# Flamingo layer on one core: weight units stored from ScalarE's queue, one tile prepared per turn, quarter-tile stores, another order of down products, scatters of the next group first

## The reference, cut to what matters

```python
# x, ctx: 32 sequences of 128 tokens, width 512, float32
xn = layernorm(x)
q  = rms_norm(xn @ Wq.T + bq) * nq            # 16 heads of 32
k  = rms_norm(ctx @ Wk.T + bk) * nk
v  = ctx @ Wv.T + bv
x  = x + tanh(g0) * (softmax(q k^T / sqrt(32)) v @ Wo.T + bo)

h  = layernorm(x)
s  = relu(h @ up) ** 2 @ down                 # 512 -> 2048 -> 512
m  = (h @ expert) * (sum of the 2 largest of h @ gate)
x  = x + tanh(g1) * (layernorm(s + m) * gamma + beta)
```

## Time and profile before

| | us |
|---|---|
| median of 3 runs | 1365.26 |
| lowest, highest | 1364.36, 1367.47 |
| the profiled execution | 1362.92 |
| its span | 1361.1 |
| attention part | 0 to about 566 |
| feed-forward, first products to end | about 566 to 1361 |
| last result of DVE | 1351.2 |

### The profile page before, as it was taken

One profiled execution on the slowest core, in us unless ns is written; L12 is line 12 of the kernel. 1 busy time (PEld: TensorE's weight loads), 2 busy tenths in 40 slices (PEclk: granted clock), 3 DMA queues, 4 the chain that ended last, 5 costly groups with the idle time before them and its releaser, 6 DMA issues.

```text
span 1361.1 us, 26319 instructions
## 1 busy us (share of the span) xinstructions
PE 1277.8 (94%) x9154; PEld 1093.8 (80%) x9154; DVE 943.1 (69%) x1568; ACT 755.8 (56%) x2012; POOL 591.3 (43%) x720
## 2 busy tenths in 40 slices
PE   7999999999899999999999999899999899999993
PEld 5887777777777778788899888799888789887993
DVE  6777777777766876665598665697664896366676
ACT  5877777777666757656455343454343543444440
POOL 3766666666655996463034322043311233111033
PEclk9999999999899999999999999899999999999997
DMA  6588888988878864659675687675677664564861
GB/s 226 140 211 222 220 221 222 231 221 213 218 200 196 205 153 115 228 220 237 233 238 177 225 234 221 202 227 176 239 227 223 220 188 165 193 221 153 230 184 62
DMA packets 335460, 276.96 MB, mean 203 GB/s; under 512 B 233852, under 2 KB 248316, under 8 KB 330239
## 3 DMA queue, kind: packets, MB, share of 16 engines
q1 hardware_dynamic: 297600, 165.79, 45.1%
q10 hardware_dynamic: 37758, 109.85, 24.6%
HBM read 198.79 MB, written 76.81 MB: 202 GB/s over the span
## 4 chain that ended last, share of the span: by engine, by line
PE 49%; DVE 16%; DMA 11%; SPq 7%; issue 6%; POOL 5%; ACT 3%; DVEq 0%; POOLq 0%; ACTq 0%
PE wide L79 15%; PE wide L80 14%; PE wide L81 14%; DMA kd_scratch<-kf 6%; SPq L1649 4%; DVE wo_lo L2006 4%; DMA k_dealt<-kd_scratch 3%; PE wide L418 2%; DMA out_x<-fxy 2%; ACT prob L817 1%; PE wide L406 1%; DVE S L1990 1%; POOL fxy L1447 1%; POOL prob L988 1%; PE wide L1728 1%
## 5 line engine op out<-in xcount | busy, mean ns | idle before, releaser
L817 ACT ACTIVATE prob<-wide,nmx 128x128 f32<-128x128 f32 x512 | 180.7, 396 | 6.0 <-DVE nmx L626 5.9
L988 POOL TENSOR_TENSOR prob<-prob,rr 128x512 f32<-128x512 f32 x128 | 136.1, 1075 | 103.9 <-DVE rr L634 103.9
L79 PE MATMUL wide<-eight,wo_hi 128*128 128x256 f32 x480 | 138.0, 288 | 12.5 <-DVE wo_lo L2006 8.3
L1820 ACT ACTIVATE hid<-wide 128x512 f32<-128x512 f32 x96 | 57.4, 599 | 156.6 <-PE wide L81 156.6
L80 PE MATMUL wide<-eight,wo_hi 128*128 128x256 f32 x480 | 136.4, 284 | 0.0
L81 PE MATMUL wide<-eight,wo_lo 128*128 128x256 f32 x480 | 136.3, 284 | 0.0
L2006 DVE TENSOR_TENSOR wo_lo<-hid,wo_hi 128x512 fp32r<-128x512 f32 x120 | 94.6, 810 | 43.6 <-ACT wo_hi L1820 43.6
L817 ACT ACTIVATION_READ_ACCUMULATOR prob<-wide,nmx 128x1 f32 x512 | 121.1, 236 | 0.0
L1820 ACT ACTIVATE wo_hi<-hid 128x512 fp32r<-128x512 f32 x120 | 74.4, 631 | 79.2 <-PE wide L81 79.2
L79 PE MATMUL wide<-wq_hi,eight 128*128 128x512 f32 x192 | 82.9, 432 | 27.1 <-DVE eight L565 27.1
L79 PEld LDWEIGHTS wide<-eight,wo_hi 128*128 128x128 f32 x480 | 92.8, 193 | 16.3 <-issue 9.4
(11 more groups left out here) (308 smaller groups left out, 3971.0 us busy)
## 6 DMA issues: line engine op xcount, KB each, us to landing
eight<-down_scratch ACTq DMA_DIRECT2D x32, 1024.0 KB, 8.0
wk_hi<-down_scratch ACTq DMA_DIRECT2D x12, 1024.0 KB, 7.8
wk_lo<-down_scratch ACTq DMA_DIRECT2D x12, 1024.0 KB, 7.5
wk_hi<-up_scratch ACTq DMA_DIRECT2D x12, 1024.0 KB, 6.8
eight<-up_scratch ACTq DMA_DIRECT2D x12, 1024.0 KB, 5.8
wk_lo<-up_scratch ACTq DMA_DIRECT2D x12, 768.0 KB, 5.6
eight<-up_scratch ACTq DMA_DIRECT2D x12, 768.0 KB, 7.0
xin<-in_x SPq DMA_DIRECT2D x32, 256.0 KB, 3.4
```

The lines of the kernel that those rows point to most:

```text
L79: eng.matmul(dst, ah, bh, start=first and k == 0, stop=False, skip_group_check=onto)
L817: i = act.activation(prob[par][:, g, h * P:(h + 1) * P], cols(bank[g], h), ACT.Exp, bias=nmx[:, n:n + 1], scale=1.0, accum_out=rs[:, n:n + 1])
L988: pool.tensor_tensor(p, p, r, ALU.mult).then_inc(po_p, 1)
L1820: return act.activation(dst, src, ACT.Copy)
```

## The change

1. **Unit stores.** SP no longer stores units. ACT does, in two parts: the raw quarters (3 of 7) at the start of the even slot, ahead of the last exponentials of the slot before, and the sums (4 of 7) at its end, after the high part of x. Semaphores are apart for the two (`st_q`, `st_qs`). Down: 2 and 2 DMAs, up: 4 and 4.
2. **First group.** One tile per slot: loads in slots 19 to 26 (four quarter DMAs each), statistics in 20 to 27, normalisation in 21 to 28 and now on DVE. Pair sums stay in slots 26 to 29, in another order. POOL keeps the reciprocal root.
3. **Groups.** SP in a group g > 0: `load_x(g+1)` first, residual tiles, seven deals, then store and residual of tiles 0 and 1, the eighth deal, tiles 2 and 3, then the four others. The statistics of the next group move from q = 1, 2 to q = 0, 1, the normalisation from 3, 4 to 2, 3; statistics of y to q = 4 to 7; results 0 to 3 to q = 5, 6.
4. **Quarter tiles.** Output stores, residual loads and the load of `last_res` are four DMAs of 32x512 in place of one of 128x512, and there is one semaphore per output tile. For the last group SP stores the first two quarters of each tile and ACT the other two.
5. **Down products.** Operand order is hid0, squared hid2, S2, S1, hid1, S4, hid3; S4 is formed in `hid`, at the steps of `SUM4_AT`, and `SUMS_AT` and `HI_AT` are later. Arithmetic and counts are the same.
6. **End.** For the last group DVE adds the epsilon to the variance and POOL only takes the power.

```diff
@@ slot on SP, on ACT
-                    if ff.third_of(s, par) is not None:
-                        ff.unit_store(sp, ff.third_of(s, par))
+                    if ff.third_of(s, par) is not None:
+                        ff.unit_store_raw(act, ff.third_of(s, par))
...
+                    if ff.third_of(s, par) is not None:
+                        ff.unit_store_sums(act, ff.third_of(s, par))
@@ slot on DVE, on POOL
+                    if ff_turn(s, TILE_DONE, ff.TILES) is not None:
+                        ff.normalise(dve, 0, ff_turn(s, TILE_DONE, ff.TILES))
+                    if ff_turn(s, TILE_STATS, ff.TILES) is not None:
+                        ff.stats(dve, 0, ff_turn(s, TILE_STATS, ff.TILES))
...
-                            ff.inv_std(pool, 0, tile)
-                            ff.normalise(pool, 0, tile)
@@ store_out
-        eng.dma_start(ff.dealt_rows(out[g * GB + i]), y[i]).then_inc(ff.st_o[i % HB], DMA)
+        for src, dst in ff.quarters(y[i], out[g * GB + i]):
+            eng.dma_start(dst, src).then_inc(ff.st_o[i], DMA)
@@ weigh
-            at_least(act, ff.st_o[j % HB], 2 * g * DMA)
+            at_least(act, ff.st_o[j], g * KT * DMA)
@@ fill_b on DVE
-                for tile in {1: range(HB), 2: range(HB, GB)}.get(q, ()):
+                for tile in {STATS_AT(g): range(HB), STATS_AT(g) + 1: range(HB, GB)}.get(q, ()):
                     ff.stats(dve, g + 1, tile)
@@ tables
-    SUMS_AT = (28, 30, 32, 34)
+    SUM4_AT = (20, 22, 24, 26, 28, 29, 30, 32)
+    SUMS_AT = (34, 37, 40, 42)
+    Y_AT = {4: (0, 1), 5: (2, 3), 6: (4, 5), 7: (6, 7)}
+    def STATS_AT(g):
+        return 1 if g == 0 else 0
```

More of the change, by code:

```diff
@@ L1396, in quarters, with load_consts @@
         return [(tile[m * P // KT:(m + 1) * P // KT, :], rows.rearrange("(b c) n -> c b n", c=KT)[m]) for m in range(KT)]
+    TILES, PAIRS = (2, 3, 0, 1, 6, 7, 4, 5), (2, 3, 0, 1)
     def load_first(sp, n):
-        if n == 0:
+        if TILES[n] == 0:
             sp.wait_ge(ql, 2 * NU)
+        if TILES[n] == 6:
             sp.wait_ge(st_q, UNITS_STORED)
[L1402 to L1410, removed]
+            sp.wait_ge(st_qs, UNITS_STORED)
+        for dst, src in quarters(y[TILES[n]], x2_dram[TILES[n]]):
+            sp.dma_start(dst, src).then_inc(ld_x[TILES[n] % HB], DMA)
+    def load_consts(sp):
+        sp.wait_ge(ga_zeroed, 1)
+        sp.dma_start(ga[:, :, 0:NE], t["gate"].rearrange("p (k n) -> p k n", k=KT)).then_inc(ld_g, DMA)
+        for src, dst in (("gamma", gamma), ("beta", beta)):
+            sp.dma_start(dst[:, :], t[src].broadcast_to([P, D])).then_inc(ld_g, DMA)
     def x_tile(g, tile):
@@ L1633, in store_out, with store_half @@
         eng.wait_ge(ff.dv_o, GB * g + i + 1)
-        eng.dma_start(ff.dealt_rows(out[g * GB + i]), y[i]).then_inc(ff.st_o[i % HB], DMA)
+        for src, dst in ff.quarters(y[i], out[g * GB + i]):
+            eng.dma_start(dst, src).then_inc(ff.st_o[i], DMA)
+    def store_half(eng, i, half):
+        eng.wait_ge(ff.dv_o, GB * LAST + i + 1)
+        for src, dst in ff.quarters(y[i], out[LAST * GB + i])[2 * half:2 * half + 2]:
+            eng.dma_start(dst, src).then_inc(ff.st_o[i], DMA)
     @block.sync
@@ L1685, in group @@
                         ff.piece_load(sp, q + 5)
-                if g > 0 and q in (2, 5):
-                    for i in range(2 * (q // 5), 2 * (q // 5) + 2):
-                        store_out(sp, g - 1, i)
-                        load_res(g - 1, i + HB)
-                if more and q in (4, 5):
-                    for tile in range(HB * (q - 4), HB * (q - 3)):
-                        deal(g + 1, tile)
+                if q in (4, 5):
+                    for tile in range(HB * (q - 4), HB * (q - 3)):
+                        deal(1, tile)
@@ new lines, in first_group, with later_group @@
+            ff.piece_store(sp, NQ)
+            ff.piece_store(sp, NQ + 1)
+        def later_group(g):
+            more = g < LAST
+            if more:
+                load_x(g + 1)
+            for i in range(HB):
+                load_res(g - 1, i)
+            if more:
+                for tile in range(GB - 1):
+                    deal(g + 1, tile)
+            for i in range(HB):
+                store_out(sp, g - 1, i)
+                load_res(g - 1, i + HB)
+                if more and i == 1:
+                    deal(g + 1, GB - 1)
+            for i in range(HB, GB):
+                store_out(sp, g - 1, i)
@@ L1693, in group @@
+        for g in range(NG8):
             if g == 0:
[L1694 to L1699 removed]
+                first_group()
+            else:
+                later_group(g)
+            if g < LAST:
                 for i in range(GB):
                     fetch(g + 1, i)
[L1702 to L1705 removed]
@@ L1707, in _ @@
-        for g in range(NG8):
-            group(g)
-        for i in (0, 1, 2, 3, 4, 6):
-            store_out(sp, LAST, i)
-        for n in range(HB):
-            sp.wait_ge(ff.st_o[n], 2 * NG8 * DMA)
+        sp.wait_ge(ff.pe_E, GB * NG8)
+        for i in range(GB):
+            for dst, src in ff.quarters(res(LAST, i), x2_dram[LAST * GB + i]):
+                sp.dma_start(dst, src).then_inc(ff.ld_r[i % HB], DMA)
+        for i in range(GB):
+            store_half(sp, i, 0)
+        for n in range(GB):
+            sp.wait_ge(ff.st_o[n], NG8 * KT * DMA)
@@ L1785, in down_part @@
             return mm3(pe, bank[m % 2 * HB + j][:, 0:H], [(hi[:, cols], lo[:, cols])], [(w[:, 0:H], w[:, H:D])],
-                       first=q == 0 and m in (0, 1, 5), last=q == NQ - 1, onto=m in (2, 3, 4, 6))
+                       first=q == 0 and m in (0, 1, 3), last=q == NQ - 1, onto=m in (2, 4, 5, 6))
         def last_product(g):
@@ L1944, in _ @@
             group(g)
-        store_out(act, LAST, 5)
-        store_out(act, LAST, 7)
+        for i in range(GB):
+            store_half(act, i, 1)
     @block.vector
@@ L2161, in group @@
                     ff.expert_lo(pool, NQ, ff.u_b)
+            if g > 0:
+                for i in range(HB, GB):
+                    residual(g - 1, i)
             if g < LAST:
```

194 lines of the change are left out of this document (101 added, 93 removed).

## The result

| | before | after |
|---|---|---|
| median of four runs each, us | 1365.9 | 1301.7 (1300.9 to 1305.3) |
| span of the profiled execution, us | 1361.1 | 1300.2 |
| first gate products of groups 0, 1, 2, 3, us | 587.6, 776.5, 972.9, 1169.2 | 539.0, 734.0, 929.1, 1116.7 |
| last gate to end of span, us | 191.8 | 183.5 |

The ratio is 0.9535, with an interval of 0.9513 to 0.9556. The kernel is faster by 64 us where 38 were forecast; the span, which the sum was made against, is 60.9 shorter. The forecast of 1327 had the direction, and the time fell out of the range of 1312 to 1347 at the fast end.

What follows compares the result with a forecast made beforehand. PE, busy 94% of the span, was taken as the bound, so its waits are time. Terms -24.4 - 6 + 2 - 15 + 14 - 2 - 6.5 = -37.9 took 1365.3 to 1327.4 us; 8-in-10 range 1312 to 1347.

Steps and rivals of the forecast that it cites:

- Unit stores: Attention: moving them to ACT's queue shortens ten slot pairs from 34.64 to 32.2 us, 24.4 us saved.
- PE would give two odd slots, 31.76: Attention: PE's bound for a pair of slots, taken as two odd slots of 15.88 us.
- The second bound: Attention: DMA engines have 29.5 us of work a pair and reach a share of 0.92, so 32.0 us.
- stands behind 1.75 MB on SP's queue: Attention, even slots: why the deal of `kf` takes 7.41 us; the unit store is ahead of it.
- a rival to which the forecast gave 0.05: Attention: ACT is blocked at its store issues, pairs last 37.8 us, time 1383 us; chance 0.05.
- The DMA engines give nothing: Attention: rival that the queue change saves only SP's issue time, 5 in place of 24.4 us, time 1347; chance 0.19.
- First group: Preparation, one tile per slot: 6 us saved in slots 26 and 27, 2 charged for DVE's added work.
- `weigh`: Feed-forward groups 1 and 2: its wait goes, 7.45 + 7.4 = 15 us saved; rival that it stays, 1342, chance 0.10.
- SP is through with seven deals before q = 5: Groups 1 and 2: scatters first finish before the first two results are ready, helping save 15 us.
- Statistics at q = 0: Groups 1 and 2: PE stalls 5.7 and 4.1 us, 14 lost with clock; no-stall rival 1313, chance 0.13.
- Down products: Feed-forward: spreading the sums cuts PE's waits for DVE, 2 us saved in all, between 0 and 8.
- The end: Last output store: 3.3 us in place of 9.9 saves 6.6; with DVE's small costs, 6.5 taken.

Runs made afterwards that it cites:

- e2: Kernel after with all four unit stores issued by SP again, at once, just ahead of the deal of kf: 1348.2 us, 0.9862.
- e1c: Kernel before with all four stores of a unit issued by ScalarE together at the slot's start: 1350.3 us, 0.9899.
- e1: Kernel before with only the unit stores moved to ScalarE, raw half at the slot's start and sums half later: 1321.8 us, 0.9676.
- e2c: Kernel after with unit stores on SP but spread, raw half ahead of the deal of kf, sums half last in the slot: 1311.7 us, 0.9592.
- e8: Kernel after with the old order of the seven down products and old places of the fourth and turned sums: 1310.9 us, 0.9585.
- e10: Kernel after with later groups' work in its old order, but quarter stores, per-tile semaphores and product order as changed: 1286.9 us, 0.9437.
- e7: Kernel after with ScalarE's first write to an output tile waiting for the stores of both tiles of the old pair: 1303.6 us, 0.9532.
- e6: Kernel after with each output tile stored by one DMA again, one semaphore per tile kept: 1312.4 us, 0.9597.
- e3: Kernel after with the next group's statistics at q = 1 and 2 and normalisation at q = 3 and 4 in every group: 1287.0 us, 0.944.
- e5: Kernel after with every store of a down unit written a second time, into an unread spare area: 1336.9 us, 0.9808.

## Why the prediction was right and wrong

**Unit stores: wrong size, and a mechanism that was right in part.** The forecast took 32.2 us for a pair, 24.4 in all; the store move alone brought 41.0 to gate 0. The step that failed is "PE would give two odd slots, 31.76". An odd slot's 15.88 us were not PE's work for a slot: PE did 150 matmuls in it and 116 in the even one, so a cut at SP's deals does not divide PE's work evenly; the kernel after, with no deal late, still has 149 and 120. A slot without a store has 15.09 us of work, with 131. The rows allowed a better sum: PE is busy for 15.88 + 16.07 = 31.95 us in the pair, and a granted clock of 0.91 over 18.39 us is up to 1.66 us of full speed lost. That gives 30.3, and 30.21 was measured. The second bound, a share of 0.92 as the most that the DMA engines reach, failed as well: they show 1.01, and up to 285 GB/s.

The mechanism, that the deal of `kf` "stands behind 1.75 MB on SP's queue", holds as far as this: the deal took 7.41 us to land there, 6.1 in e2 (at 200.64), and 3.3 in the kernel after. But it is not the whole of it. The rest is near a rival to which the forecast gave 0.05: an engine is held at its issues. SP was held at `x_dealt` for 4.35 us before, and DVE waited 3.22 us for that tile and then 1.42 us for `k_dealt`; the two are not separated. ScalarE was held too where it issued all four stores in a row (e1c). So the gain hangs on the store being split, spread over the pair and kept from right ahead of the deal, and little on the engine that issues it. No run has the whole burst right ahead of the deal but on the other queue, so whether the deal was late by its place in the queue or by the bytes beside it stays open. The 1.2 us of issues charged at nothing were rightly hidden: the profile of after shows the two issues of a half at 0.38 and 0.41 us, and beside ScalarE's 12.8 us of idle time at issues from 60 to 470 us PE waits for 2.5 us in all.

**The DMA engines give nothing, 0.19: refuted**, by e1. The sentence of the Trainium skill that was weighed with it ("DMA: Bandwidth & Descriptors", Issuing engines are not separate DMA queues), that another issuer saves only the time to start the DMAs, would have given 5 us. The measured 44 decide against that use of it, though not against what it says. Most of the 44 come from splitting and spreading the stores and not from the other issuer: with all of them on SP but spread, three quarters of the gain stay (e2c).

**First group: net 4 forecast, some 7.6 measured.** The step that was off is the 6 us for slots 26 and 27: the last six slots fell by 10.1 us from e1 to the kernel after. POOL is busy for 12.92 us in the slot that had 17.92, as forecast. The 2 us charged for VectorE's work beside the unit work were due, and the four slots with both grew by 3.6.

**`weigh`: the gain came as forecast, its reason was wrong.** Without the stall the intervals 1 to 2 and 2 to 3 are 9.8 and 8.6 shorter than before; 7.45 and 7.4 were forecast, and the products account for 0.4 and 1.1 us of the rest (e8). But the step "SP is through with seven deals before q = 5" is not needed (e10), and neither is the tile's own semaphore (e7) or the quarter stores (e6). Each of these runs keeps the two other edits, so any two of the three are enough. No run has one of them alone, so which of them would be enough by itself stays open.

**Statistics at q = 0: right mechanism, and nearly the size.** Stalls of 5.7 and 4.1 us were forecast and 6.0 and 6.8 came, with the clock 14 against 17 by the intervals (e3), inside the bound of 20. Group 2 was missed by 2.7 us: the step took 9.0 us for the landing of the last load, and the longest of that group now takes 11.8, so VectorE's last wait ends 15.0 us after `collect` and not 12.2. What slows the load is not shown; the step had named the residual loads, which now stand right behind it on SP.

**Down products: 2 forecast, 6.0 measured** (e8), inside the bounds of 0 to 8. PE's waits for these low parts fell from 8.3 us in the kernel before to 1.8. I had seen some 8 of them and taken most of the gain back for the stretch behind, and no new wait of PE of that size arose there.

**The end: 6.5 forecast, 6.7 measured**, 9.9 to 3.2.

Of the 23 us between -37.9 and -60.9 of span, 16.6 are the stores, 3.6 the first group, 4 the products and 2 the weighing; 3 more of stall go the other way. These are single executions: see the scatter of gate 0 at the end, which is as large as the smaller of these terms.

## What to carry to other kernels

To bound what a freed stretch will last, take PE's busy time over the whole pattern (both slots of the pair), less what a reduced clock accounts for, and not one part of it, since a cut between the parts need not divide PE's work evenly. Before moving large DMAs to another engine, ask how many stand in a row and what stands behind them: two at a time cost nothing here on ScalarE, 10 us in all on SP ahead of the deal (e2c), and four in a row held ScalarE for 3 us each time. Work that waits for fresh loads does not belong ahead of the operation that PE needs next: one constant in the changed kernel, undone, gives 1287.0 us, the fastest here with the old order of the later groups (1286.9).

## What the runs showed of the hardware

- Four DMAs of 384, 384, 512 and 512 KB in a row took ScalarE 0.38, 0.38, 0.66 and 1.42 us to issue, and left it idle for 2.99 us (e1c). On SP the same four took 0.42, 0.39, 0.56 and 0.88, the deal behind them 1.27 and `x_dealt` 2.78 (e2). Two of 896 KB on SP took 0.42 and 0.41, the deal 1.23 and `x_dealt` 4.35 (before).
- A deal of 256 KB landed in 7.4 us right behind 1.75 MB on its own queue (before), in 4.8 behind 0.75 MB (e2c), and in 3.3 with no store right ahead of it (e1).
- DMA shares of 1.01 and 0.94 went with 259 and 243 GB/s (after), 1.04 and 1.00 with 285 and 268 (e5). The share alone does not give the rate.
- Kernels with the same attention code (after, e3, e6, e7, e8, e10) have gate 0 at 539.0, 539.2, 541.1, 541.6, 544.4 and 540.1 us. Differences of a few us are to be read from gate to gate, not from the whole span.
